# A language-model layer on one core: the score banks become a ring of three pairs, all other TensorE jobs share one PSUM bank, and the order of work is rewritten

## The chip, the core and the metric

The kernel runs on one core of a Trainium2 chip. Its engines work through queues of their own, each in order: TensorE (PE in the profile, its weight loads PEld), VectorE (DVE), ScalarE (ACT), GpSimd (POOL) and SyncE (SP, transfers only). They wait for one another through semaphores. The metric is the device time of one execution in microseconds, as the median of several runs.

## The reference

Inputs are token numbers (8, 1024), a segment label, tables, and the weights of one transformer layer of width 192, with 12 heads of 16 and a hidden width of 768.

```python
h = segment_row + position + token_row          # (8, 1024, 192)
x = layernorm(h)
q, k, v = split(x @ qkv_weight.T)               # 12 heads of 16
q, k = layernorm(q) * 16**-0.5, layernorm(k)    # over each head's 16
h = h + (softmax(q k^T) @ v) @ proj_weight.T    # 1024 x 1024 scores, 8 x 12 times
x = layernorm(h)
x = round(clip(x / mean(alpha_a1), -8, 7)) @ wq1.T   # quantised weights
x = clip(gelu(x * alpha_w1 * mean(alpha_a1) + b1), -10, 10)
x = round(clip(x / mean(alpha_a2), -8, 7)) @ wq2.T
h = h + x * alpha_w2 * mean(alpha_a2) + b2
```

## The kernel before

The 8 x 1024 positions are cut into 16 halves of 512 positions (`HALVES`), and each half into four tiles of 128 (`TH`). The kernel goes through a short start, 16 half-steps and a tail. Half-step s does the attention of the 512 queries of half s against all 1024 keys. It consists of 24 units: a unit (u) is one group of four heads with one tile of 128 keys. For each unit TensorE writes four score matrices (`scores`, L1212) in two pairs of PSUM banks (`ps_s`, four banks), ScalarE takes the Exp of each pair (`exps`, L679) into one of four buffers `probs`, and TensorE multiplies by v (`heads`, L1232) into the bank `ps_o`. That last step stands two units behind (`HEADS_BEHIND`). A pair of score banks is written again once its last Exp is done.

All other work is laid between the units by hand: the text `PLAN` (L77) has a line for each of the 24 units, and each engine reads from it, in order, the words that concern it. A word is a letter with the tile's number. Capital letters of `JOB_KINDS` are TensorE jobs that write a PSUM bank of their own, and VectorE copies or uses the result when its queue comes to the same word: A turns the normed input, B makes q and k, C makes v, D and E turn q and k, F turns the attention's output and divides it by the row sums, G turns it back, H projects it and adds it to h, I turns the quantised input, X is the first feed-forward product (then Gelu on ScalarE), Y the second, W turns weights (in half-step 1 alone). Further words are VectorE's own: P and l are row statistics, R the reciprocal roots of both of them in one chain of 11 small linked operations, N and m apply the norms, r sums squares, S takes the 96 roots for q and k, n splits q and k into high and low halves, x quantises a Gelu block, o copies `ps_o`. h stands for a unit of `heads` on TensorE, g marks the place of the six Gelus on ScalarE (`GELU_UNIT`), which loads the Gelu table before them and the Exp table after.

In half-step s these jobs work on different halves (`LAG`): P, N and A to E on half s+2, F to I and X on s-1, Y on s-2. So half-steps 1 to 13 have all of A to E, 14 and 15 have none.

The jobs go round three PSUM banks `ps_j` (`bank_of`, L208): X on two of them in turn, B on the third, the rest in the order of the plan. A job waits until the last result in its bank has been taken out (`job_before`, L220). PSUM has eight banks: 4 + 1 + 3.

GpSimd has its own fixed order in each half-step (`one`, L608):

```python
add_result(s0, s)            # waits for all four Y tiles, two additions
ahead = s0 + GATHER_AHEAD    # 3
if FIRST_GATHERED <= ahead < HALVES:     # half-steps 1 to 12
    add_segments(ahead)      # four gathers, then a wait for them to land
    add_tokens(ahead)        # four gathers
square(s0, s)                # for each tile: waits for B's copy; r waits for it
split_low(s0, s)             # low halves: waits for n; D and E wait for it
```

`link` makes VectorE wait until its own operation has finished, before the next that reads it.

## Time and profile before

| | |
|---|---|
| median of 3 runs | 1070.18 us (1068.22 to 1071.05) |
| span of the profiled execution | 1067.6 us, nothing beside it is listed |
| TensorE matmuls busy | 979.4 us (92%) |
| ScalarE busy | 872.6 us (82%) |
| VectorE busy | 813.9 us (76%) |
| GpSimd busy | 411.8 us (39%) |
| longest waits | TensorE's score weight loads for the Exp, 267.6 us in 420 waits; ScalarE's Exp for scores, 120.6 us in 183 |

Busy time of TensorE contains the overlap of matmuls in its pipeline, so 92% doesn't mean that it runs at its peak. The profile is of one execution, and the sums below are made against its span.

### The profile page before, as it was taken

The page shows a single profiled execution, that of the slowest core. Times are in us where ns is not written, and L with a number is a line of the kernel's source. Part 1 is how long each engine was busy: PE and PEld are TensorE (multiplying, and loading weights), DVE is VectorE, ACT ScalarE, POOL GpSimd, SP SyncE. Part 2 cuts the span into 40 slices and gives each one's busy share as a digit, 9 for nine tenths or more (in the row PEclk, how much of TensorE's full clock was granted, in tenths as well). Part 3 has the DMA queues.
Part 4 walks back from the last instruction along what each step waited for, and adds up shares of the span by engine and source line. Part 5 has one row for each costly group of instructions (what it writes and reads, how often), then busy time and mean ns, then how long its engine had stood idle before and what let it go on. Part 6 is the DMA issues. An engine that isn't in the chain of part 4 may idle for free.

```text
span 1067.6 us, 19577 instructions
## 1 busy us (share of the span) xinstructions
PE 979.4 (92%) x7571; PEld 389.1 (36%) x7571; DVE 813.9 (76%) x2325; ACT 872.6 (82%) x950; POOL 411.8 (39%) x345
## 2 busy tenths in 40 slices
PE   5589999999999999999999999999999999989885
PEld 4333433334342433434343343434334343413223
DVE  5878869788686969878696977869697886825347
ACT  1387788897979889797988979798888989798883
POOL 6555513635343353534435363443526412201000
PEclk9899999999999999999999999999999999999997
DMA  7511200303011040202102040110202000000000
GB/s 162 127 16 16 31 1 2 46 1 64 12 25 22 1 75 1 38 8 58 18 2 45 1 73 3 31 16 16 30 1 45 1 16 1 16 1 1 16 1 31
DMA packets 25762, 28.62 MB, mean 27 GB/s; under 512 B 5027, under 2 KB 22182, under 8 KB 25670
## 3 DMA queue, kind: packets, MB, share of 16 engines
q0 software_dynamic: 16896, 11.80, 9.4%
q1 hardware_dynamic: 8624, 15.55, 4.8%
q8 instruction: 61, 1.00, 0.4%
q14 instruction: 31, 0.25, 0.1%
q10 hardware_dynamic: 150, 0.01, 0.0%
HBM read 21.06 MB, written 6.29 MB: 26 GB/s over the span
## 4 chain that ended last, share of the span: by engine, by line
PE 40%; ACT 30%; DVE 24%; issue 3%; POOL 3%; DMA 0%
ACT probs L682 22%; PE ps_o L1247 12%; PE ps_s L1227 8%; PE ps_j L1271 4%; ACT gelu L676 4%; PE ps_j L1279 3%; PE ps_j L1325 3%; POOL stack L592 3%; PE ps_j L1286 2%; PE ps_j L1292 2%; ACT L676 2%; ACT L682 2%; DVE hn L797 2%; PE ps_j L1311 2%; PE ps_j L1296 2%
## 5 line engine op out<-in xcount | busy, mean ns | idle before, releaser
L682 ACT ACTIVATE probs<-ps_s 128x1024 f32<-128x1024 f32 x768 | 736.1, 1023 | 125.5 <-PE ps_s L1227 120.6
L1247 PE MATMUL ps_o<-probs,v_sb 128*32 128x512 f32 x3072 | 394.7, 605 | 0.2 <-DVE o_sb L859 0.2
L1227 PE MATMUL ps_s<-qT,kT 64*128 64x512 f16 x1536 | 264.3, 384 | 35.0 <-ACT probs L682 25.2
L592 POOL TENSOR_TENSOR stack<-sq,stack 128x384 f16<-128x384 f32 x124 | 120.5, 992 | 162.9 <-DVE stack L846 162.9
L1227 PEld LDWEIGHTS ps_s<-qT,kT 64*128 64x128 f16 x1536 | 61.5, 93 | 299.5 <-ACT probs L682 267.6
L525 POOL DMA_INDIRECT h_all<-in_L_tok_token_table,idx x60 | 96.7, 1611 | 59.5 <-DMA h_all<-in_L_tok_segm_table,idx 41.2
L1247 PEld LDWEIGHTS ps_o<-probs,v_sb 128*32 128x32 f32 x3072 | 69.1, 109 | 124.3 <-issue 116.1
L601 POOL TENSOR_TENSOR y_sb<-y_sb,b_row 128x768 f32<-128x768 f32 x14 | 25.4, 1814 | 198.8 <-DVE y_sb L931 198.8
L581 POOL TENSOR_TENSOR sq<-qk 128x384 f32<-128x384 f32 x56 | 46.2, 826 | 139.5 <-DVE qk L894 139.5
L525 POOL DMA_INDIRECT h_all<-in_L_tok_segm_table,idx x56 | 87.2, 1557 | 15.2 <-issue 13.1
L1279 PE MATMUL ps_j<-wh,partsT 128*128 128x384 f16 (+1 forms) x384 | 71.5, 296 | 1.0 <-ACT partsT L663 0.7
L1286 PE MATMUL ps_j<-ident_h,stack 128*128 128x128 f16 x768 | 61.2, 224 | 11.8 <-POOL stack L592 10.4
L676 ACT ACTIVATE gelu<-ps_j,b_sb,s_sb 128x512 f32<-128x512 f32 x90 | 65.3, 773 | 7.5 <-PE ps_j L1311 6.7
L894 DVE TENSOR_SCALAR qk<-ps_j,w_back 128x384 f32<-128x384 f32 x56 | 34.6, 618 | 48.1 <-PE ps_j L1279 48.0
L1286 PEld LDWEIGHTS ps_j<-ident_h,stack 128*128 128x128 f16 x768 | 45.6, 100 | 50.1 <-issue 39.3
L859 DVE COPY o_sb<-ps_o 128x512 f32<-128x512 f32 x47 | 32.0, 680 | 41.4 <-PE ps_o L1247 41.4
L846 DVE CAST stack<-sq 128x384 f16<-128x384 f32 x128 | 58.7, 500 | 2.2
L878 DVE TENSOR_SCALAR gelu<-gelu,ia,qlo 128x512 f32<-128x512 f32 x90 | 58.4, 648 | 0.0
L1311 PE MATMUL ps_j<-xqT,w1T 96*128 96x512 bf16 x180 | 52.9, 388 | 3.7 <-ACT gelu L676 2.7
L1279 PE MATMUL ps_j<-wl,partsT 128*128 128x192 f16 (+1 forms) x256 | 54.3, 295 | 0.0
L879 DVE TENSOR_SCALAR gelu<-gelu,qhi 128x512 f32<-128x512 f32 x90 | 50.8, 565 | 3.2
L1271 PE MATMUL ps_j<-wpT,oT 96*128 96x192 f32 x240 | 45.7, 333 | 0.0
(201 smaller groups left out, 1118.5 us busy)
## 6 DMA issues: line engine op xcount, KB each, us to landing
out<-h_all SPq DMA_DIRECT2D x15, 384.0 KB
h_all<-in_positions SPq DMA_DIRECT2D x7, 768.0 KB
gelu<-in_L_ffn_w SPq DMA_DIRECT2D x2, 576.0 KB
h_all<-in_L_tok_token_table,idx POOLq DMA_INDIRECT x60
h_all<-in_L_tok_segm_table,idx POOLq DMA_INDIRECT x56
probs<-in_L_attn_qkv_weight SPq DMA_DIRECT2D x2, 432.0 KB, 4.7
h_all<-in_positions SPq DMA_DIRECT2D x2, 384.0 KB, 8.0
o_nat<-in_L_ffn_alpha_a SPq DMA_DIRECT2D x1, 384.0 KB
```

What stands on the lines that cost most here:

```text
L525: nc.gpsimd.indirect_dma_start(out=h_tile(half, j), out_offset=None, in_=table, in_offset=bass.IndirectOffsetOnAxis(ap=idx[:, which, t:t + ...
L592: last = nc.gpsimd.tensor_tensor(low, src, high, ALU.subtract)
L676: nc.scalar.activation(gelu[:, j], bank(("X", j), s0), ACT.Gelu, bias=b1_sb[:, j:j + 1], scale=s1_sb[:, j:j + 1]).then_inc(job_out["X"], 1)
L682: nc.scalar.activation(probs[:, u % PROBS, 2 * pair:2 * pair + 2], ps_s[:, 2 * pair:2 * pair + 2], ACT.Exp, scale=SCORE_SCALE).then_inc(ex ...
L846: last = nc.vector.tensor_copy(high, src)
L878: link(ts(gelu[:, t], gelu[:, t], ia2[:], qlo[:], ALU.mult, ALU.max))
L1227: last = mm(ps_s[:, j], kT[rows, par, head // 2, m * P:(m + 1) * P], qT[rows, par, head // 2, nh * NQ:(nh + 1) * NQ], start=True, stop=True)
L1247: last = mm(ps_o[32 * j:32 * j + 2 * D, :], v_sb[:, par, m, (GH * group + j) * VE:(GH * group + j) * VE + 2 * D], probs[:, u % PROBS, j], ...
L1271: last = mm(ps[:, 0:C], oT[:, t, k], wpT[:, k], start=(k == 0), stop=(k == 1))
L1279: last = mm(ps[:, 0:hi - lo], partsT[:, t, m], w, start=(n == 0), stop=(n == len(passes) - 1))
L1286: last = nc.tensor.transpose(bank16((kind, t), s0, F16)[:, i * P:(i + 1) * P], src, ident_h[:])
L1311: last = mm(ps, w1T[:, k, t * P:(t + 1) * P], xqT[:, k], start=(k == 0), stop=(k == 1))
```

## The change

The eight PSUM banks are divided anew: 6 + 1 + 1. `ps_s` becomes a ring of three pairs. The pairs of scores and the three pairs of X (`hidden`) take its places in turn (`RING_ORDER`); `ring_free` makes an entry wait for the one three places before it. All other jobs share the single bank `ps_j` from half-step 1 on. Half-step 0 and the start keep three job banks (two of them lie in the ring's third pair) and their order.

Jobs are merged over tiles from half-step 1 on (`TILES`): A, C, G, H and Y do two tiles in one job with one copy, I all four; `count` converts the semaphore counts. The roots R are split into R for the first norm and Q for the second; the norms N and m are done in two halves each. The Gelus come one unit after the mark g. The plan is written anew.

```diff
 PLAN = """
-h h o
-Y0 Y1 Y2 F0 Y3 F1
-G0 F2 F3 H0 G1 P0
-h h
-G2 G3 W0 W1 W2 H1 H2 H3
-h l0 h R0
-W3 m0 h
-W4 h
-h N0 W5 I0
-I1 h o A0
-I2 h A1 A2
-h A3 I3
-C0 B0 X0
-X1 B1 r0 X2 X3 B2 X4 X5 r1 B3 h r2 h r3 g h
+h h o P0
+Y0 F0 R0
+h Y1 N0
+h F1 F2 N1
+h F3 A0
+h G0 A1
+h B0 r0 G1
+h B1 r1 W0
+H0 h W1
+h o B2 r2 W2
+h H1 W3
+h B3 r3 l0 W4
+h S0 W5
+h Q0 n0
+h m0 m1 C0
+h I0 n1 D0
+X0 h E0 n2 X1 D1 h X2 o g E1 n3 C1
+D2 x0 E2
+h D3 x1
+h E3 x2
+h x3
+h x4
+h x5
 h
-h S0 n0
-h n1 o
-D0 x0 E0 C1
-n2 h C2 D1
-E1 n3 h
-D2 h x1
-h D3 E2 x2
-E3 x3 x4 h
-x5 C3 h
 """
...
-JOBS = [w[:2] for unit in UNIT_WORK for w in unit if w[0] in JOB_KINDS]
-GELU_UNIT = next(u for u, unit in enumerate(UNIT_WORK) if ("g", 0, 0) in unit)
+JOBS = [w[:2] for unit in UNIT_WORK for w in unit if w[0] in JOB_KINDS and w[0] != "X"]
+GELU_UNIT = next(u for u, unit in enumerate(UNIT_WORK) if ("g", 0, 0) in unit) + 1
...
 BANKS = 3
-IN_TURN = [w for w in JOBS if w[0] not in "XB"]
+PAIRS = 3
+TILES = {"A": 2, "C": 2, "G": 2, "H": 2, "Y": 2, "I": 4}
+FIRST_MERGED = {"A": 3, "C": 3}
+LAST_MERGED = {"G": HALVES - 1, "H": HALVES - 1, "I": HALVES - 1, "Y": HALVES - 2}
+RING_ORDER = [entry for u in range(HG * TB)
+              for entry in ([("X", 0), ("X", 1), ("X", 2)] if u == GELU_UNIT else []) + [("S", 2 * u), ("S", 2 * u + 1)]]
...
 def bank_of(job, s0):
-    kind, t = job
-    if s0 <= 0:
-        return START_JOBS.index((job, s0)) % BANKS
-    return {"X": t % 2, "B": 2}[kind] if kind in "XB" else IN_TURN.index(job) % BANKS
+    return START_JOBS.index((job, s0)) % BANKS if s0 <= 0 else 0
...
+def tiles_of(kind, s0):
+    return TILES.get(kind, 1) if s0 >= 1 else 1
...
-        ps_s = ctx.enter_context(nc.psum_tensor("ps_s", [P, GH, NQ], F32))
+        ps_s = ctx.enter_context(nc.psum_tensor("ps_s", [P, 2 * PAIRS, NQ], F32))
         ps_o = ctx.enter_context(nc.psum_tensor("ps_o", [P, NQ], F32))
-        ps_j = ctx.enter_context(nc.psum_tensor("ps_j", [P, BANKS, 512], F32))
+        ps_j = ctx.enter_context(nc.psum_tensor("ps_j", [P, 512], F32))
+        def job_bank(n):
+            return (ps_j[:], ps_s[:, 4], ps_s[:, 5])[n]
...
+        def ring(s0, entry):
+            return entry[1] % 2 if s0 == 0 else RING_ORDER.index(entry) % PAIRS
...
-            def norm_roots(s0):
-                lo = 0 if job_runs("P", s0) else 1
-                hi = 2 if job_runs("H", s0) else 1
-                if lo < hi:
-                    rsqrt(rn[:, lo:hi], vn[:, lo:hi], wn[:, lo:hi])
-            def first_norm(s0, s):
+            def norm_roots(which):
+                rsqrt(rn[:, which], vn[:, which], wn[:, which])
+            def first_norm(s0, s, i):
                 half = job_half("N", s)
                 if s0 == -2:
@@ -793,12 +833,13 @@
                 if s0 <= 0:
                     dve.wait_ge(job_mm["A"], (s + 2) * TH)
-                for t in range(TH):
+                here = slice(0, TH) if s0 <= 0 else slice(2 * i, 2 * i + 2)
+                for t in range(TH)[here]:
                     last = ts(hn[:, t], h_tile(half, t), mv[:, 0, t, 0:1], rn[:, 0, t:t + 1],
                               ALU.subtract, ALU.mult)
                 link(last)
-                link(nc.vector.tensor_copy(parts[:, :, 0:C], hn[:]))
-                tt(parts[:, :, C:2 * C], hn[:], parts[:, :, 0:C], ALU.subtract).then_inc(hn_ready, 1)
+                link(nc.vector.tensor_copy(parts[:, here, 0:C], hn[:, here]))
+                tt(parts[:, here, C:2 * C], hn[:, here], parts[:, here, 0:C], ALU.subtract).then_inc(hn_ready, 1)
...
-            def second_norm(s0, s):
+            def second_norm(s0, s, i):
                 half = job_half("I", s)
-                link(ts(ra2[:], rn[:, 1], ia1[:], None, ALU.mult))
-                for t in range(TH):
+                if i == 0:
+                    link(ts(ra2[:], rn[:, 1], ia1[:], None, ALU.mult))
+                here = slice(2 * i, 2 * i + 2)
+                for t in range(TH)[here]:
                     last = ts(xf[:, t], h_tile(half, t), mv[:, 1, t, 0:1], ra2[:, t:t + 1],
                               ALU.subtract, ALU.mult)
                 link(last)
-                quantise(xq[:], xf[:], xf[:], QN, QP).then_inc(xq_ready, 1)
+                quantise(xq[:, here], xf[:, here], xf[:, here], QN, QP).then_inc(xq_ready, 1)
...
+                    two = h_all[:, at:at + 2 * C]
+                    tt(two, ps[:, 0:2 * C], two, ALU.add).then_inc(job_out["H"], 1)
...
+            def ring_free(s0, s, entry):
+                if s0 == 0:
+                    if entry[1] >= 2:
+                        pe.wait_ge(exp_done, entry[1] - 1)
+                    return
+                at = RING_ORDER.index(entry)
+                if at >= PAIRS:
+                    (kind, n), step = RING_ORDER[at - PAIRS], s
+                elif s0 >= 2:
+                    (kind, n), step = RING_ORDER[at - PAIRS], s - 1
+                elif at < 2:
+                    (kind, n), step = ("S", 2 * UNITS - 2 + at), s - 1
+                else:
+                    for bank_n in (1, 2):
+                        (pk, pt), step = [j for j in START_JOBS if bank_of(*j) == bank_n][-1]
+                        pe.wait_ge(job_out[pk], count(pk, job_half(pk, step), pt))
+                    return
+                if kind == "S":
+                    pe.wait_ge(exp_done, 2 * UNITS * step + n + 1)
+                else:
+                    pe.wait_ge(job_out["X"], count("X", job_half("X", step), 2 * n + 1))
...
+            def hidden(s0, s, i):
+                half = job_half("X", s)
+                if i == 0:
+                    pe.wait_ge(job_out["I"], count("I", half, TH - 1))
+                ring_free(s0, s, ("X", i))
+                for j in (2 * i, 2 * i + 1):
+                    for k in range(2):
+                        last = mm(ps_s[:, 2 * ring(s0, ("X", i)) + j % 2], w1T[:, k, j * P:(j + 1) * P], xqT[:, k],
+                                  start=(k == 0), stop=(k == 1))
+                    last.then_inc(job_mm["X"], 1)
```

The `nth(...)` counts in all waits on jobs become `count(...)`; the start's and the tail's uses of the banks go through `job_bank`. Start, tail and half-step 0 are otherwise as they were.

## Rows read from the trace of the kernel before

**Rows 1.** Timeline of ScalarE: start us, us, engine, operation
```profile
458.10 1.28 ACT L676 ACT_TABLE_LOAD   x1
...
464.25 1.28 ACT L682 ACT_TABLE_LOAD   x1
...
465.55 11.46 ACT L682 ACTIVATE probs<-ps_s 128x1024 f32<-128x1024 f32 x12
...
519.68 1.28 ACT L676 ACT_TABLE_LOAD   x1
```

**Rows 2.** Windows, one half-step: busy us of PE, PEld, DVE, ACT, POOL
```profile
458.10:519.68 61.58, 58.89 (x470) 22.86 (x468) 49.62 (x140) 52.92 (x56) 27.28 (x22) 1.00 0.18 33
```

**Rows 3.** Timeline of TensorE
```profile
463.03 0.66 PE L1279 MATMUL ps_j<-wh,partsT 128*128 128x384 f16 x3
...
463.95 2.78 PE L1247 MATMUL ps_o<-probs,v_sb 128*32 128x512 f32 x24
...
477.35 0.61 PE L1227 MATMUL ps_s<-qT,kT 64*128 64x512 f16 x4
...
477.88 0.51 PE L1286 MATMUL ps_j<-ident_h,stack 128*128 128x128 f16 x6
...
500.18 2.16 PE L1271 MATMUL ps_j<-wpT,oT 96*128 96x192 f32 x12
```

**Rows 4.** Groups of VectorE: count, busy us, mean ns, idle before
```profile
L894 DVE TENSOR_SCALAR qk<-ps_j,w_back 128x384 f32<-128x384 f32 x56 | 34.6, 618 | 48.1 <-PE ps_j L1279 48.0
...
L859 DVE COPY o_sb<-ps_o 128x512 f32<-128x512 f32 x47 | 32.0, 680 | 41.4 <-PE ps_o L1247 41.4
...
L918 DVE TENSOR_TENSOR o_nat<-ps_j,rsum 128x192 f32<-128x192 f32 x60 | 21.4, 357 | 2.1
```

**Rows 5.** Timeline of VectorE
```profile
466.20 0.21 DVE L831 TENSOR_SCALAR vq<-vq 128x96 f32<-128x96 f32 x1
...
469.57 0.56 DVE L841 TENSOR_TENSOR sq<-qk,rq 128x384 f32<-128x384 f32 x1
...
470.16 0.63 DVE L846 CAST stack<-sq 128x384 f16<-128x384 f32 x2
...
471.29 1.95 DVE L846 CAST stack<-sq 128x384 f16<-128x384 f32 x2
...
502.77 0.35 DVE L768 BATCH_NORM_STATS2 st<-h_all 128x6 f32<-128x192 f32 x1
...
504.86 0.17 DVE L745 TENSOR_SCALAR wn<-vn 128x8 int32<-128x8 int32 x1
...
507.43 1.25 DVE L870 TENSOR_SCALAR o_nat<-h_all,mv,ra 128x192 f32<-128x192 f32 x4
...
509.78 1.31 DVE L797 TENSOR_SCALAR hn<-h_all,mv,rn 128x192 f32<-128x192 f32 x4
```

**Rows 6.** Timeline of GpSimd
```profile
494.42 1.81 POOL L601 TENSOR_TENSOR y_sb<-y_sb,b_row 128x768 f32<-128x768 f32 x1 [11.10 <-DVE y_sb L931]
...
498.28 1.54 POOL L525 DMA_INDIRECT h_all<-in_L_tok_segm_table,idx  x1
...
508.83 1.84 POOL L525 DMA_INDIRECT h_all<-in_L_tok_token_table,idx  x1 [3.47 <-DMA h_all<-in_L_tok_segm_table,idx]
...
514.66 1.54 POOL L525 DMA_INDIRECT h_all<-in_L_tok_token_table,idx  x1 [0.30 <-issue]
...
520.35 0.82 POOL L581 TENSOR_TENSOR sq<-qk 128x384 f32<-128x384 f32 x1 [4.15 <-DVE qk L894]
```

**Rows 7.** Timeline and windows of TensorE, with the granted clock
```profile
28.11 0.48 PE L1299 MATMUL ps_j<-ident_h,parts 128*128 128x128 f16 x3 [9.59 <-DVE parts L791]
...
512.83 0.33 PE L1299 MATMUL ps_j<-ident_h,parts 128*128 128x128 f16 x3 [0.37 <-DVE parts L801]
...
30.00:35.00 5.00, 5.00 (x18) 2.54 (x19) 3.73 (x17) 2.62 (x6) 4.39 (x3) 1.00 1.10 246
...
45.00:50.00 5.00, 3.00 (x28) 2.52 (x26) 4.86 (x11) 1.93 (x3) 2.57 (x2) 0.50 0.04 15
```

More of the change, by code:

```diff
@@ L208, in bank_of, with count @@
 def bank_of(job, s0):
-    kind, t = job
-    if s0 <= 0:
-        return START_JOBS.index((job, s0)) % BANKS
-    return {"X": t % 2, "B": 2}[kind] if kind in "XB" else IN_TURN.index(job) % BANKS
+    return START_JOBS.index((job, s0)) % BANKS if s0 <= 0 else 0
+def count(kind, half, t):
+    per, tiles = PER_HALF[kind], TILES.get(kind, 1)
+    whole = min(half, FIRST_MERGED.get(kind, 0))
+    merged = max(min(half, LAST_MERGED.get(kind, HALVES)) - whole, 0)
+    rest = half - whole - merged
+    own = tiles if whole == FIRST_MERGED.get(kind, 0) and half < LAST_MERGED.get(kind, HALVES) else 1
+    return (whole + rest) * per + merged * (per // tiles) + t // own + 1
+def tiles_of(kind, s0):
+    return TILES.get(kind, 1) if s0 >= 1 else 1
 def jobs_of(s0):
@@ L576, in square @@
                 for t in range(TH):
-                    pool.wait_ge(job_out["B"], nth(half, t, TH))
+                    pool.wait_ge(job_out["B"], count("B", half, t))
                     if job_half("B", s0) > 2 or t >= 2:
@@ L656, in copy_out @@
                 half = job_half(kind, s)
-                act.wait_ge(job_mm[kind], nth(half, t, TH))
+                act.wait_ge(job_mm[kind], count(kind, half, t))
                 if kind == "B":
@@ L674, in gelu_out @@
                 half = job_half("X", s)
-                act.wait_ge(job_mm["X"], nth(half, j, HB))
-                nc.scalar.activation(gelu[:, j], bank(("X", j), s0), ACT.Gelu, bias=b1_sb[:, j:j + 1],
+                act.wait_ge(job_mm["X"], count("X", half, j))
+                nc.scalar.activation(gelu[:, j], ps_s[:, 2 * ring(s0, ("X", j // 2)) + j % 2], ACT.Gelu, bias=b1_sb[:, j:j + 1],
                                      scale=s1_sb[:, j:j + 1]).then_inc(job_out["X"], 1)
@@ L885, in job_result @@
                 half, h0 = job_half(kind, s), job_half(kind, s0)
-                job = (kind, t)
+                job, first = (kind, t), t * tiles_of(kind, s0)
                 ps = bank(job, s0)
@@ L890, in job_result @@
                         continue
-                    dve.wait_ge(job_mm[kind], nth(half, t, TH))
+                    dve.wait_ge(job_mm[kind], count(kind, half, first))
                     if kind in "BC":
@@ L1258, in job @@
                     (pk, pt), ps_step = prior
-                    pe.wait_ge(job_out[pk], nth(job_half(pk, ps_step), pt, PER_HALF[pk]))
+                    pe.wait_ge(job_out[pk], count(pk, job_half(pk, ps_step), pt * tiles_of(pk, ps_step)))
                 ps = bank((kind, t), s0)
+                tiles = range(t * tiles_of(kind, s0), (t + 1) * tiles_of(kind, s0))
                 if kind == "A":
@@ L1263, in job @@
                         pe.wait_ge(hn_first, t + 1)
-                    elif t == 0:
+                    elif s0 <= 0 and t == 0:
                         pe.wait_ge(hn_ready, half)
+                    elif s0 >= 1:
+                        pe.wait_ge(hn_ready, 2 + 2 * (half - 3) + t + 1)
                 if kind == "B":
-                    pe.wait_ge(job_out["A"], nth(half, t, TH))
+                    pe.wait_ge(job_out["A"], count("A", half, t))
                 if kind == "H":
-                    pe.wait_ge(job_out["G"], nth(half, t, TH))
-                    for k in range(2):
-                        last = mm(ps[:, 0:C], oT[:, t, k], wpT[:, k], start=(k == 0), stop=(k == 1))
+                    pe.wait_ge(job_out["G"], count("G", half, tiles[0]))
+                    for n, tile in enumerate(tiles):
+                        for k in range(2):
+                            last = mm(ps[:, n * C:(n + 1) * C], oT[:, tile, k], wpT[:, k], start=(k == 0), stop=(k == 1))
                 if kind in "BC":
@@ L1277, in job @@
                     passes = [(m, high[:, m]) for m in range(KP)] + [(m, low[:, m]) for m in range(KP - 1)]
-                    for n, (m, w) in enumerate(passes):
-                        last = mm(ps[:, 0:hi - lo], partsT[:, t, m], w, start=(n == 0), stop=(n == len(passes) - 1))
+                    for i, tile in enumerate(tiles):
+                        for n, (m, w) in enumerate(passes):
+                            last = mm(ps[:, i * C:i * C + hi - lo], partsT[:, tile, m], w,
+                                      start=(n == 0), stop=(n == len(passes) - 1))
                 if kind in "DE":
```

161 lines of the change are left out of this document (92 added, 69 removed).

## The prediction

> **What bounds the kernel now.** I read the windows first: one steady half-step. The two ScalarE table loads that open the Gelu blocks of two successive half-steps stand at 458.10 and 519.68 [rows 1], so a half-step takes 61.6 us. In it TensorE is busy 58.9, ScalarE 52.9, VectorE 49.6 and GpSimd 27.3 us [rows 2]. Then the timeline of ScalarE: a table load and six Gelus from 458.10 to 464.25, so the load 1.28 and the Gelus with their waits 4.9, table load 1.28, then Exps at 0.955 us each (twelve in 11.45) [rows 1]. 48 Exps and this block make 53, so ScalarE idles 8.6 us of 61.6. TensorE's rows carry the rest: four score matmuls 0.54 us (477.35 to the transposes at 477.88), the head matmuls of one unit (eight passes) 0.93 in a row (2.78 for three units), some 1.0 alone, a B job 0.9, three H tiles 2.1 [rows 3]. No one engine is full. The half-step is set by how four in-order queues interlock, so I ask of the new PLAN where each queue stands behind another one.
>
> **The change part by part.**
>
> *The ring of three score pairs.* PE may now write the scores of pair n once Exp n-3 is done, before n-2. That lets it run about one Exp (0.96 us) further ahead. It pays where PE jobs come in lumps: at most that 8.6 us of ScalarE idling, over 15 half-steps. It gives nothing where PE itself waits in its own queue, since the scores stand behind the waiting job.
>
> *One job bank.* Back-to-back jobs are serial: hand-over to VectorE 0.2, copy 0.6 (618 ns for 384 columns [rows 4]), hand-over back 0.15, so about 1 us of PE wait when nothing lies between. Twelve or so such neighbours stand in the new PLAN. Those after F1, F2, F3, G0 and B0 cost 4 to 5 us by this price, but two longer waits, below, take most of them in.
>
> *Merging.* Two tiles in one copy save 0.1 to 0.2 us on VectorE (2 x 357 ns for 192 columns against 618 for 384 [rows 4]), 1 to 2 us per half-step. A second root chain costs 2.3 us more (504.86 to 507.43, less 0.26 for the scaling at its end [rows 5]), halved norms 0.5. VectorE stays near 50 us: a draw. It matters only through the order.
>
> *The new order,* which carries the forecast. I walk one steady half-step as a closed path, time 0 being F0 on TensorE in unit 1.
>
> a) F0 0.33 and its VectorE part 0.6 (product 0.36 [rows 4], reciprocal and link 0.25) with hand-overs: 1.15. VectorE then does R0, 2.3, and only then copies Y1 (0.55): the last y is out at **4.0**.
>
> b) GpSimd works its queue in order: add_result, the eight gathers of a later half, and only then the squares. In the trace it starts adding at 494.42, when the last y is out; the segment gathers begin at 498.28, the token gathers at 508.83 after a wait for the former to land; the last begins at 514.66 and takes 1.54, so it is free at 516.2, 21.8 us after the last y [rows 6]. Before, the first square was wanted at 520.35, when GpSimd had already sat idle 4.15 us. In the new PLAN B0 and r0 stand in unit 6, four units after Y1. TensorE reaches the end of B0 at about 16 on my path (Y1 1.0, two F, A, G0 and five times scores and heads of 1.54, with the bank waits). The square can start only at 25.9. VectorE sits in r0, behind it the copy of G1, behind that, in the only job bank, B1. So r0 ends 21.8 + 0.8 square + 0.55 reduce + 0.2 = **23.35** later.
>
> c) Copy of G1 and hand-over: **0.8**.
>
> d) TensorE from B1 to the end of B3, units 7 to 11: three B 2.55, two merged H 2.8, four scores 2.2, four heads 4.0, bank wait between B1 and H0 0.35: **11.9**. ScalarE needs 7.7 for these four units, so PE leads.
>
> e) From B3's end to I0. VectorE's queue there is r3, l0, S0, Q0, n0, m0, m1, then the copy of C0, which frees the bank. Before, S0 started 2.25 us after B3's last matmul (463.95 to 466.20 [rows 5, 3]); l0 takes 2.1 (502.77 to 504.86), S0 3.4 (466.20 to 469.57), Q0 2.2, n0 1.15, m0 and m1 2.35 (507.43 to 509.78) plus 0.7 for the halving [rows 5], C0's copy and hand-over 0.75. Beside m0 GpSimd makes the low parts: such a pair of casts took 1.95 instead of 0.6 [rows 5], so 1.4 more. Sum **16.3**. Over it TensorE has four units of scores and heads and C0, 7.1 us, ScalarE 7.7: neither covers it. PE stands about 9 us at I0 and ScalarE runs dry, because the scores of unit 16 stand behind I0 and D0.
>
> f) I0 0.7, its copy and hand-overs 1.05, D0 0.45, scores to the first Exp 0.45, two Exps 1.95, table load, six Gelus, table load 7.0 (7.4 before, with 0.47 of waiting): **11.6**.
>
> g) Fourteen Exps, to the end of unit 23: **13.4**. PE has 1.5 to 1.9 us per unit against 1.92: ScalarE bounds, as in the long run after 465.55 [rows 1].
>
> h) Heads of unit 23 wait for the last Exp, 1.15; copy o 0.68 [rows 4], statistics P0 1.95, Y0's copy and hand-over 0.7: F0 may start after **4.5**. P0 before Y0's copy is new; it puts 2 us on the path.
>
> Sum: 4.0 + 23.35 + 0.8 + 11.9 + 16.3 + 11.6 + 13.4 + 4.5 = 85.9.
>
> *The clock.* In the steady half-step the granted clock is 1.00 [rows 2]. In the prologue PE stood 9.59 us before 28.11 and then needed 0.48 for three transposes that take 0.33 later; in 45 to 50 us, after the next gap, the clock is 0.50 [rows 7]. The path above has two gaps of some 9 us, in b and e. The rows show about 5 us of dense work at 1.2 GHz until it recovers. After b PE is on the path: +2.6. After e: I0, D0 and scores at half speed +1.7, and the last Gelu pair comes late by another 1.3: +3.0. Below, nothing (the clock may hold); above, double.
>
> So a half-step takes 91.5, 29.9 more than before. That holds for half-steps 2 to 12, eleven of them: +329. Half-step 13 gathers nothing: r0 follows B0 at once, 9.0 less in b and no clock loss of 2.6: +18. Half-step 1 adds no result, and its gathers are early enough: +18 too, and the six W jobs, each in the one bank with a 0.68 copy, +5. Half-steps 14 and 15 have no A to E and none of b's or e's queue: the ring gains some 2 us each, -4. Half-step 0 and the tail keep their order: 0. 1067.6 + 329 + 18 + 23 - 4 = 1433.6, and 2.6 for the median of the runs over this span: **1436**.
>
> The Trainium skill, in "SBUF — State Buffer", section "Who interferes with whom", says that VectorE's two-port operations and GpSimd exclude each other for a whole instruction, whoever comes first. By that rule m0's first operations would wait one or two GpSimd subtractions, 0.9 to 1.8 us in place of my 1.4. The trace agrees in size: +1.35 for the pair of casts [rows 5].
>
> The same skill, in "PSUM — Partial Sum Buffer", section "Summary: rules for kernel authors", advises to write a different bank while one is read. It speaks against the single job bank. By the row's turnaround of 1 us, twelve neighbours would cost up to 12 us per half-step and the time would be at most 1250 if that were all; the two queues in b and e are dearer and cover most of it.
>
> **Rivals.** *The clock holds* over the two gaps: 11 x 5.6 + 2 x 3 = 68 less, 1368. For it: the windows of 25 to 35 us, whose matmuls were slow, are listed at full clock [rows 7], so the link between gap and speed is loose. *GpSimd's queue is no wait*: TensorE comes to B0 so late, or the gathers start so early, that the squares are ready. Then b shrinks to 14.35 and 11 x (9.0 + 2.6) = 128 fall away: 1308. Against: add_result waits for Y1 itself, so only a stretch Y1 to B0 of 22 us would do it. *Both queues are longer*: VectorE's operations beside the gathers, or half speed for 10 us: up to 11 x 5.6 more, 1500. *Faster*: the waits of b and e are covered, the third pair evens the lumps out and only TensorE's 58.9 us [rows 2] count: 2.7 x 14 = 38 less, 1032. It decides if Y1 to B0 plus the VectorE queue of e shrink by over 24 us; ScalarE's idle 8.6 us speak for a gain, the two queues against it. *The change does nothing to the pace*: excluded but for chance, since the order itself changes.
>
> **Numbers.** Forecast 0.58; clock holds 0.17; GpSimd hidden 0.08; longer 0.08; somewhere between 1080 and 1290 by overlaps I missed 0.03; faster 0.05; same 0.01. The range 1290 to 1490 takes in the first three and part of the fourth, 0.85. The measurement tells about 0.3%, 3 us, from no change. Slower 0.94, same 0.01, faster 0.05.
>
> **What would show it.** Right: Gelu loads about 91 us apart in the middle, near 80 for half-steps 1 and 13, 60 or less in the last two; VectorE waiting 8 to 9 us in the reduce of r0 for the square, once per half-step; GpSimd with no idle time between its last gather and its first square; ScalarE idle over 8 us twice per half-step; clock at 0.5 in windows after the gaps. Wrong: a GpSimd square that waits for qk as before, an I0 that starts within 10 us of B3, or a steady clock.

## The result and the profile after

| | before | after |
|---|---|---|
| median of the runs | 1069.3 us (1068.2 to 1071.1) | 1418.3 us (1412.2 to 1421.2, 4 runs) |
| profiled execution, span | 1067.6 us | 1419.5 us |
| granted clock of TensorE, mean | 0.983 | 0.88 |

The ratio is 1.325, 95% interval 1.321 to 1.329: 349 us slower. The window of one half-step of the changed kernel, between two Gelu table loads (busy us of PE, PEld, DVE, ACT and POOL, then the granted clock), answers to [rows 2]:

```profile
540.10:629.75 89.65, 67.16 (x469) 23.95 (x468) 52.10 (x141) 52.58 (x57) 26.49 (x22) 0.86 0.10 14
```

The half-step is 28.1 us longer. ScalarE and GpSimd are busy about as long as before (52.6 and 26.5 us) and VectorE 2.5 us longer. TensorE is busy 8.3 us longer over practically the same matmuls (469 and 470); its granted clock is 0.86 where it was 1.00. The other 20 us are waits. ScalarE's timeline shows where (the idle time before a row in brackets; compare [rows 1]):

```profile
566.57 1.94 ACT L725 ACTIVATE probs<-ps_s 128x1024 f32<-128x1024 f32 x2 [1.70 <-PE ps_s L1299]
...
576.23 1.94 ACT L725 ACTIVATE probs<-ps_s 128x1024 f32<-128x1024 f32 x2 [5.09 <-PE ps_s L1299]
...
595.27 1.94 ACT L725 ACTIVATE probs<-ps_s 128x1024 f32<-128x1024 f32 x2 [5.69 <-PE ps_s L1299]
...
627.79 1.94 ACT L725 ACTIVATE probs<-ps_s 128x1024 f32<-128x1024 f32 x2 [10.82 <-PE ps_s L1299]
629.75 1.28 ACT L718 ACT_TABLE_LOAD   x1
...
636.98 1.28 ACT L725 ACT_TABLE_LOAD   x1
```

In its three longest waits for scores (5.09, 5.69 and 10.82 us) TensorE itself stands still, each time for VectorE. TensorE's timeline (compare [rows 3] for B, H and the scores at full speed):

```profile
565.66 0.55 PE L1370 MATMUL ps_j<-ident,o_sb 128*128 128x128 f32 x3 [1.45 <-DVE y_sb L976]
...
574.75 0.90 PE L1370 MATMUL ps_j<-ident,o_sb 128*128 128x128 f32 x3 [3.90 <-DVE o_nat L961]
...
592.90 1.14 PE L1356 MATMUL ps_j<-wh,partsT 128*128 128x384 f16 x3 [4.09 <-DVE oT L939]
...
595.58 2.93 PE L1347 MATMUL ps_j<-wpT,oT 96*128 96x192 f32 x8
...
605.06 1.57 PE L1347 MATMUL ps_j<-wpT,oT 96*128 96x192 f32 x8
...
609.01 0.60 PE L1299 MATMUL ps_s<-qT,kT 64*128 64x512 f16 x4
...
624.52 1.09 PE L1386 MATMUL ps_j<-ident_b,xq 128*96 128x128 bf16 x8 [8.32 <-DVE v_sb L937]
```

These are F0, F2, B1, H0, H1, the scores behind B3, and I0. The reason for the gap at B1 is read from GpSimd's timeline (compare [rows 6]) and then VectorE's:

```profile
569.59 1.88 POOL L643 TENSOR_TENSOR y_sb<-y_sb,b_row 128x768 f32<-128x768 f32 x1 [20.60 <-DVE y_sb L976]
...
573.50 1.54 POOL L567 DMA_INDIRECT h_all<-in_L_tok_segm_table,idx  x1
...
583.75 1.53 POOL L567 DMA_INDIRECT h_all<-in_L_tok_token_table,idx  x1 [3.16 <-DMA h_all<-in_L_tok_segm_table,idx]
...
589.27 1.54 POOL L567 DMA_INDIRECT h_all<-in_L_tok_token_table,idx  x1 [0.30 <-issue]
590.25 1.42 POOL L623 TENSOR_TENSOR sq<-qk 128x384 f32<-128x384 f32 x1
```

```profile
569.43 2.16 DVE L838 TENSOR_SCALAR hn<-h_all,mv,rn 128x192 f32<-128x192 f32 x2
571.63 1.94 DVE L841 CAST parts<-hn 128x384 f16<-128x384 f32 x1
...
576.23 0.73 DVE L838 TENSOR_SCALAR hn<-h_all,mv,rn 128x192 f32<-128x192 f32 x2
576.99 0.36 DVE L841 CAST parts<-hn 128x384 f16<-128x384 f32 x1
...
591.70 0.55 DVE L865 TENSOR_REDUCE vq<-sq 128x24 f32<-128x384 f32 x1 [5.12 <-POOL sq L623]
592.17 0.68 DVE L939 COPY oT<-ps_j 96x512 f32<-96x512 f32 x1
```

GpSimd squares only when its eight gathers are through; VectorE waits 5.12 us in r0 with the copy of G1 behind it, and B1 waits for that copy. The first two rows (N0) against the next two (N1) also show a wait that the prediction did not have: beside GpSimd's two additions, N0 took 4.1 us for what N1 does in 1.1. F1's copy stands behind N0 in VectorE's queue, and F2 needs the one bank that this copy frees, hence F2's 3.90 us.

Over the whole program: the Gelu loads of half-steps 2 and 12 stand at 274.66 and 1168.38, 89.4 us per half-step against 61.6. The Gelus stand five units later in the new order, so for single half-steps I count from the first Exp of one to the first Exp of the next. By that measure the 352 us between the two spans are 24 in half-step 1 (87.4 against 63.4), 307 in half-steps 2 to 12 (984.2 against 677.6 together), 20.5 in half-step 13 (81.6 against 61.1) and less than 1 in half-steps 14 and 15 together. Half-step 0 and the tail take as long as before.

### The profile page after: what moved, and what is told of

It is laid out like the page before. It is cut to its first block, busy times and chain, and to the rows that moved or that the text cites. A ratio compares the mean times of both kernels' runs of the same rounds, so it can differ in the third digit from the quotient of the medians.

```text
span 1419.5 us, 19572 instructions
## 1 busy us (share of the span) xinstructions
PE 1079.6 (76%) x7571; PEld 399.3 (28%) x7571; DVE 843.1 (59%) x2339; ACT 866.9 (61%) x950; POOL 402.9 (28%) x345
## 4 chain that ended last, share of the span: by engine, by line
PE 39%; DVE 27%; POOL 15%; ACT 9%; issue 9%; DMA 1%; POOLq 0%; DVEq 0%
PE ps_o L1319 13%; POOL h_all L567 10%; ACT probs L725 8%; PE ps_s L1299 6%; PE ps_j L1347 4%; PE ps_j L1364 4%; PE ps_s L1414 4%; PE ps_j L1356 4%; DVE o_nat L913 2%; DVE st L811 2%; POOL sq L623 2%; DVE stack L887 2%; DVE sq L882 2%; POOL y_sb L643 1%; POOL h_all L647 1%
## 5 line engine op out<-in xcount | busy, mean ns | idle before, releaser
L1319 PE MATMUL ps_o<-probs,v_sb 128*32 128x512 f32 x3072 | 434.8, 645 | 1.3 <-DVE o_sb L900 0.8
L634 POOL TENSOR_TENSOR stack<-sq,stack 128x384 f16<-128x384 f32 x124 | 113.1, 933 | 312.3 <-DVE stack L887 312.3
L1299 PEld LDWEIGHTS ps_s<-qT,kT 64*128 64x128 f16 x1536 | 51.1, 95 | 210.9 <-ACT probs L725 144.3
L1386 PE MATMUL ps_j<-ident_b,xq 128*96 128x128 bf16 x120 | 15.4, 305 | 105.2 <-DVE v_sb L937 105.2
L1370 PE MATMUL ps_j<-ident,o_sb 128*128 128x128 f32 x180 | 38.2, 329 | 69.0 <-DVE o_nat L961 50.3
L865 DVE TENSOR_REDUCE vq<-sq 128x24 f32<-128x384 f32 x56 | 31.0, 553 | 95.4 <-POOL sq L623 95.4
L937 DVE TENSOR_SCALAR qk<-ps_j,w_back 128x384 f32<-128x384 f32 x54 | 33.4, 618 | 75.3 <-PE ps_j L1356 75.3
L718 ACT ACTIVATE gelu<-ps_s,b_sb,s_sb 128x512 f32<-128x512 f32 x90 | 64.2, 774 | 14.3 <-PE ps_s L1414 14.0
L939 DVE COPY kT<-ps_j 128x768 f16<-128x768 f16 x54 | 30.0, 556 | 63.0 <-PE ps_j L1364 63.0
L1347 PE MATMUL ps_j<-wpT,oT 96*128 96x192 f32 x240 | 60.2, 406 | 1.1 <-DVE w1T L946 0.9
L1356 PEld LDWEIGHTS ps_j<-wh,partsT 128*128 128x128 f16 x342 | 26.4, 101 | 118.3 <-DVE oT L939 56.8
```

The source lines that it names most:

```text
L634: last = nc.gpsimd.tensor_tensor(low, src, high, ALU.subtract)
L718: nc.scalar.activation(gelu[:, j], ps_s[:, 2 * ring(s0, ("X", j // 2)) + j % 2], ACT.Gelu, bias=b1_sb[:, j:j + 1], scale=s1_sb[:, j:j + 1] ...
L1299: last = mm(ps_s[:, at], kT[rows, par, head // 2, m * P:(m + 1) * P], qT[rows, par, head // 2, nh * NQ:(nh + 1) * NQ], start=True, stop=True)
L1319: last = mm(ps_o[32 * j:32 * j + 2 * D, :], v_sb[:, par, m, (GH * group + j) * VE:(GH * group + j) * VE + 2 * D], probs[:, u % PROBS, j], ...
L1347: last = mm(ps[:, n * C:(n + 1) * C], oT[:, tile, k], wpT[:, k], start=(k == 0), stop=(k == 1))
L1356: last = mm(ps[:, i * C:i * C + hi - lo], partsT[:, tile, m], w, start=(n == 0), stop=(n == len(passes) - 1))
```

## The experiments

Every run is compared with the kernel before on the same chip. All keep the whole computation.

**1. The gathers last in GpSimd's queue**, to take the squares out from behind them.

```diff
                 add_result(s0, s)
                 ahead = s0 + GATHER_AHEAD
+                square(s0, s)
+                split_low(s0, s)
                 if FIRST_GATHERED <= ahead < HALVES:
                     add_segments(ahead)
                     add_tokens(ahead)
-                square(s0, s)
-                split_low(s0, s)
```

> The changed kernel with one edit: GpSimd does its squares and low halves ahead of the gathers of a later half. The order theory says that VectorE's reduce r0 in unit 6 stands behind the gathers in half-steps 2 to 12. Without that wait B1 starts some 8 us earlier, and what TensorE does at half speed behind that gap is gained too, about 4 us: 11 x 12 = 130 us less, near 1285. The rival that the single job bank sets the pace says that r0 only fills time in which jobs would wait anyway: under 2% less, above 1390. If the gathers at the end hold up the next add_result or P0, some 3 us per half-step come back, near 1320.

Measured: 1435.6 us, ratio 1.343 (1.338 to 1.347): slower than the change itself. The squares come at once (first row), but the wait did not go, it moved. VectorE's, GpSimd's and TensorE's timelines:

```profile
595.86 0.55 DVE L865 TENSOR_REDUCE vq<-sq 128x24 f32<-128x384 f32 x1 [0.94 <-POOL sq L623]
...
659.29 0.35 DVE L811 BATCH_NORM_STATS2 st<-h_all 128x6 f32<-128x192 f32 x1 [5.94 <-issue]
```

```profile
654.90 1.54 POOL L567 DMA_INDIRECT h_all<-in_L_tok_token_table,idx  x1 [0.30 <-issue]
```

```profile
661.69 0.90 PE L1370 MATMUL ps_j<-ident,o_sb 128*128 128x128 f32 x3 [7.46 <-DVE y_sb L976]
```

GpSimd is through with the last token gather at 656.4, and P0's first row starts at 659.29. The profile names no releaser for that wait; I read it as the landing of the tokens, some 3 us later. P0 of the next half-step needs them and, new in this order, stands ahead of Y0's copy. So GpSimd's queue has two deadlines: squares by unit 6 and tokens by P0. The expectation had named the second one, but at some 3 us; the wait is 5.94 us. The time also lies above the rival's 1390, but not for its reason, as run 5 shows.

**2. TensorE kept at work in the gaps** of half-steps 1 to 13 by extra score matmuls (20 before F2, 24 before B1, 48 before I0), overwritten by the real scores.

```diff
+            WARM = {("F", 2): (4, 20), ("B", 1): (8, 24), ("I", 0): (16, 48)}
...
                         elif kind in job_mm:
+                            if at is None and 1 <= s0 <= 13 and (kind, t) in WARM:
+                                warm(s0, s, *WARM[kind, t])
```

> The changed kernel with score matmuls done ahead of time, and again at their place, while TensorE would stand idle: 20 ahead of F2, 24 ahead of B1, 48 ahead of I0, in half-steps 1 to 13. They fill most of the gaps and fit in them. If the half speed behind the gaps is a cost of its own, the matmuls from B1 to B3 take 12 instead of 16 us and those from I0 on 2 us less: 60 to 80 us less in all, 1340 to 1360, with a granted clock near 1. If the clock is only a sign and VectorE and GpSimd set the pace, the time stays within 1% of 1418. If the added matmuls delay the jobs behind them, it rises by up to 30.

Measured: 1392.8 us, ratio 1.307 (1.298 to 1.316), clock 0.955 in the profiled execution: 25 us faster than the change, less than expected. The four times spread more than in other runs, from 1388.5 to 1407.4. From B1 to the scores behind B3 it took 13.8 us (581.21 to 594.97) against 16.1. TensorE's timeline shows why not more:

```profile
575.73 2.76 PE L1415 MATMUL ps_s<-qT,kT 64*128 64x512 f16 x24
581.21 0.66 PE L1356 MATMUL ps_j<-wh,partsT 128*128 128x384 f16 x3 [2.71 <-DVE oT L939]
...
582.90 2.81 PE L1347 MATMUL ps_j<-wpT,oT 96*128 96x192 f32 x8 [0.17 <-DVE qk L937]
...
594.97 0.61 PE L1299 MATMUL ps_s<-qT,kT 64*128 64x512 f16 x4
...
610.47 1.09 PE L1386 MATMUL ps_j<-ident_b,xq 128*96 128x128 bf16 x8 [3.02 <-DVE v_sb L937]
```

The fillers left 2.71 and 3.02 us of gap, and H0 and I0 behind them still ran at half speed. So the clock has at least these 25 of the 349 us. It can't be the main cause: with a clock of 0.955, 323 us were left.

**3. The order of the change on nearly the old division of PSUM**: two score pairs and three job banks.

```diff
-PAIRS = 3
+PAIRS = 2
...
-    return START_JOBS.index((job, s0)) % BANKS if s0 <= 0 else 0
+    return START_JOBS.index((job, s0)) % BANKS if s0 <= 0 else JOBS.index(job) % BANKS if job in JOBS else 0
...
-        ps_j = ctx.enter_context(nc.psum_tensor("ps_j", [P, 512], F32))
+        ps_j = ctx.enter_context(nc.psum_tensor("ps_j", [P, BANKS, 512], F32))
```

One thing differs from the kernel before: X stays in the ring, beside the scores, while before it had job banks of its own.

> The changed kernel's order, merging and roots, with PSUM divided as before: two pairs in the ring (scores and X share it) and three job banks in turn. The order theory says that the division of PSUM is a minor part: B1 may pass the blocked copy of G1, I0 the copy of C0, some 5 us per half-step, against a little less lead of the scores: 1340 to 1400. If the single bank were the cause, most of the 350 us would go: under 1200.

Measured: 1395.2 us, ratio 1.304 (1.302 to 1.307). With the third pair given up for two more job banks, the kernel is 23 us faster; no run separates what the banks gain from what the pair loses. The ring is not what made the kernel slow. The Trainium skill advises to write another bank while one is read ("PSUM — Partial Sum Buffer", section "Summary: rules for kernel authors"): the runs agree in this order, by these 23 us net; run 8 shows the opposite sign in another.

**4. VectorE's queue ahead of I0 shortened**: l0, r3, Q0, C0, m0, m1, I0 ahead of S0 and n0 (units 11 to 15, each line of the plan put between bars), and the D and E jobs about one place later.

```diff
-h B3 r3 l0 W4 | h S0 W5 | h Q0 n0 | h m0 m1 C0 | h I0 n1 D0
+h B3 l0 r3 W4 | h Q0 C0 W5 | h m0 m1 I0 | h S0 | h n0 n1
...
```

> The changed kernel with VectorE's queue behind B3 in another order: l0 ahead of r3, Q0, C0's copy, m0, m1 and I0 ahead of S0 and n0, and the D and E jobs one place later. The order theory: from B3 to I0 9 to 10 us in place of 15.5, and S0 and n0 lie beside I0 and three units, so 5 to 6 us less in each of 13 half-steps: 1340 to 1350. The rival that VectorE is simply full over the half-step, so that moving its work about gives nothing: within 1% of 1418.

Measured: 1404.8 us, ratio 1.313 (1.307 to 1.318): 13.5 us faster, a fifth of the expected. From B3's end to I0 it is now 8.9 us (686.2 to 695.14) instead of 15.5, as meant. But the Exps of units 14 and 15 now come behind I0 and not ahead of it, and D0 to E1, pushed behind the Gelus, make ScalarE wait 2.22 and 1.43 us there. ScalarE still idles 5.7 us at I0, and half-steps 14 and 15, which have no A to E, got 7 us longer together (from first Exp to first Exp, 123.2 against 116.0):

```profile
628.03 1.94 ACT L725 ACTIVATE probs<-ps_s 128x1024 f32<-128x1024 f32 x2 [2.22 <-PE ps_s L1299]
631.40 1.94 ACT L725 ACTIVATE probs<-ps_s 128x1024 f32<-128x1024 f32 x2 [1.43 <-PE ps_s L1299]
...
696.78 1.94 ACT L725 ACTIVATE probs<-ps_s 128x1024 f32<-128x1024 f32 x2 [5.72 <-PE ps_s L1299]
```

**5. GpSimd's queue as add, segments, squares, tokens, low halves**: both deadlines of run 1 are met. The wait for the segments to land stands at the head of `add_tokens` in the code (and not at the end of `add_segments`, as the listing of GpSimd's order above has it), so the squares don't stand behind it.

```diff
                     add_segments(ahead)
+                square(s0, s)
+                if FIRST_GATHERED <= ahead < HALVES:
                     add_tokens(ahead)
-                square(s0, s)
                 split_low(s0, s)
```

> The changed kernel with GpSimd's queue cut otherwise: the addition, the segment gathers, the squares, then the token gathers, then the low halves. The segment gathers fit ahead of B0, the tokens between r3 and n0, so neither r0 nor the P0 of the next half-step should find GpSimd busy. The order theory: what putting all gathers last took from r0 and gave back at P0 is now kept, 8 us and some of the half-speed work per half-step, eleven times: 1290 to 1320. The rival, that r0's wait only covers other waits (the single bank, VectorE's queue): above 1390.

Measured: 1336.3 us, ratio 1.249 (1.246 to 1.252): 82 us faster than the change, though 16 us above the expected range, and 82.0 us per half-step. GpSimd's, VectorE's and TensorE's timelines (the last two rows are B1 and the scores behind B3):

```profile
629.24 1.54 POOL L567 DMA_INDIRECT h_all<-in_L_tok_segm_table,idx  x1 [0.30 <-issue]
636.80 0.83 POOL L623 TENSOR_TENSOR sq<-qk 128x384 f32<-128x384 f32 x1 [6.03 <-DVE qk L938]
```

```profile
637.67 0.55 DVE L866 TENSOR_REDUCE vq<-sq 128x24 f32<-128x384 f32 x1 [0.94 <-POOL sq L623]
```

```profile
638.89 0.66 PE L1357 MATMUL ps_j<-wh,partsT 128*128 128x384 f16 x3
...
651.02 0.60 PE L1300 MATMUL ps_s<-qT,kT 64*128 64x512 f16 x4
```

GpSimd now waits for the qk and not the other way round, and B1 to B3 take 12.1 us at full speed. This one place in the queue costs 82 us, and a time over 1390 us, which the rival gave, is refuted.

**6. Run 5 with P0 behind Y0's copy.**

```diff
-h h o P0
-Y0 F0 R0
+h h o
+Y0 P0 F0 R0
```

> As the run with the tokens behind the squares, and P0 one word later, behind Y0's copy. The statistics of 1.95 us then run beside scores and F0's wait and not ahead of Y0's copy: 1 to 2 us less in each of 13 half-steps, 13 to 26 us under that run. If VectorE's whole queue up to Y1 is what counts, P0 costs the same in either place: no difference.

Measured: 1351.4 us, ratio 1.263 (1.260 to 1.266), 15 us slower than run 5, which neither expectation had. In run 5, P0 lay beside Y0's matmuls, so it did not hold Y0's copy by its full length; behind it, it holds F0's. From the copy o to the copy of Y1 it took 6.3 us there (612.84 to 619.16) and 6.6 here (616.39 to 622.97), and F2 waits 4.62 instead of 3.90 us. So the prediction's term h (P0 ahead of Y0's copy puts 2 us on the path) named the right row but not a saving: GpSimd's addition hangs on Y1, and P0 is ahead of Y1's copy either way. Every second or third half-step is some 2.5 us longer than the others; why is not shown.

**7. Another spread order on the ring of three pairs and the one bank**, with GpSimd's queue of run 5, as in all runs that follow. The units 0 to 23, eight to a line:

```
h Y0 P0 | h | o Y1 | F0 h F1 h F2 | h R0 F3 | h | G0 h G1 N0 h H0 W0 | N1 H1 W1
A0 l0 | h B0 h W2 | o A1 Q0 h | B1 m0 r0 W3 | h B2 m1 W4 | r1 h W5 | B3 h r2 r3 | I0 S0 h
X0 h C0 n0 X1 C1 n1 X2 g h h x0 D0 | o E0 n2 | D1 h x1 | E1 n3 h | D2 h x2 E2 x3 | h D3 | h | x4 E3 x5 h
```

> The changed kernel's ring, single job bank, merging and split roots, with the tokens behind the squares and a new PLAN that spreads the jobs over the units, so that no queue stands behind a long chain of another: l0 in unit 8, Q0 in 10, m0 and m1 in 11 and 12, I0 in 14, S0 behind it, P0 and R0 in units 0 and 4. If the order is the cause and the division of PSUM and the merging cost nothing by themselves, a half-step takes 59 to 62 us and the time lies between 1030 and 1080, beside 1069. If one job bank, however well spaced, holds the jobs up, or VectorE is too full with two root chains, it stays above 1120.

Measured: 1114.6 us, ratio 1.042 (1.040 to 1.043), between the two expectations. It is 35 us above the first, but 304 of the 349 us are gone with the ring, the one bank, the merged jobs and the roots per norm all in place. What is left shows in TensorE's and VectorE's timelines:

```profile
501.70 0.82 PE L1365 MATMUL ps_j<-ident_h,stack 128*128 128x128 f16 x6 [2.99 <-DVE qT L940]
...
504.17 1.94 PE L1320 MATMUL ps_o<-probs,v_sb 128*32 128x512 f32 x8
```

```profile
493.36 0.55 DVE L883 TENSOR_TENSOR sq<-qk,rq 128x384 f32<-128x384 f32 x1
...
495.07 2.88 DVE L883 TENSOR_TENSOR sq<-qk,rq 128x384 f32<-128x384 f32 x1
...
498.53 0.54 DVE L922 TENSOR_SCALAR gelu<-gelu,ia,qlo 128x512 f32<-128x512 f32 x1
499.10 1.02 DVE L923 TENSOR_SCALAR gelu<-gelu,qhi 128x512 f32<-128x512 f32 x1
500.15 1.02 DVE L924 TENSOR_SCALAR hq<-gelu 128x512 bf16<-128x512 f32 x1
501.10 0.54 DVE L940 COPY qT<-ps_j 128x768 f16<-128x768 f16 x1
```

The copy of D0 stands behind n1, whose multiply takes 2.88 us instead of 0.55 beside two subtractions of GpSimd, and behind x0, slowed too. Then TensorE runs at half speed (0.82 us for six transposes that take 0.51 at 507.00, 1.94 for heads that take 1.07 at 507.44).

**8. Run 7 with two pairs and three job banks** (edit of run 3, order of run 7).

> The same new PLAN with PSUM divided as before: a ring of two pairs with X in it, and three job banks. It tells what the third pair is worth when no long wait stands in the way. If the ring evens out lumps of TensorE work, this is slower than the run with three pairs by 1 to 3 us per half-step, 15 to 45 us. If job banks matter more, it is faster.

Measured: 1148.1 us, ratio 1.073 (1.070 to 1.075): with X in the ring, three pairs with one bank are 33.5 us faster than two pairs with three banks in this order. It is not the division of the kernel before, whose X had job banks; no run tests that one in this order.

Counted from first Exp to first Exp, two parts of runs 3 and 8 have the same sign in both orders. In half-steps 14 and 15, without A to E, the third pair wins: 120.5 us with two pairs against 116.0 in the order of the change, and 121.6 against 113.3 in this one. In half-step 1, which has the W jobs besides, three job banks win: 76.3 against 87.4 us, and 68.7 against 75.3. Only in between does the sign hang on the order.

**9. Run 7 with D0's copy ahead of x0**, and **10. a third order**:

```diff
-X0 h C0 n0 X1 C1 n1 X2 g h h x0 D0
+X0 h C0 n0 X1 C1 n1 X2 g h h D0 x0
```

```
h | h o Y0 | F0 h F1 | F2 P0 h | G0 h | R0 Y1 h | F3 h G1 W0 | N0 H0 N1 h H1 W1
A0 h l0 | A1 h W2 | o B0 | h Q0 B1 m0 W3 | h B2 h W4 | r0 m1 B3 W5 | r1 r2 h I0 | r3 S0 h
X0 C0 X1 n0 C1 h X2 g | n1 D0 h x0 h E0 | o D1 | n2 E1 h | h x1 D2 h n3 | E2 h x2 | D3 h | x3 E3 x4 h x5
```

> The new order (1114.6 us) with two words exchanged: the copy of the first transposed Q (job D0) stands ahead of the first block of the Gelu's scaling (x0) in VectorE's queue. Theory: in each of the 13 middle half-steps TensorE waits 2.99 us for that copy, which is ready some 2.3 us earlier than VectorE comes to it, and then works at half speed for the next ~5 us (transposes of 0.82 instead of 0.51 us, heads of 1.94 instead of 1.06). With the copy ahead the gap falls under 1.5 us, the half speed goes, and a half-step is 2 to 3 us shorter: 1074 to 1092 us. Rival: the gap moves to the next wait of the same chain (the second multiply of the scaling, which takes 2.9 us beside GpSimd's low halves), or the order is close to its floor elsewhere: 1105 to 1115 us.

> The same kernel with another spread order of the same jobs (the transposes of the attention output one unit earlier, the first B job three units later, D0 ahead of x0, the words at most four in a unit but for one). It asks how much hangs on a particular order once the chain is spread. If what costs the 45 us over the kernel before is crowding at a few units, this order, whose units are more even, gives 1085 to 1110 us; if any spread order loses the same to GpSimd's and VectorE's shared reads, it gives 1110 to 1130 us.

Measured: run 9 1107.5 us, ratio 1.036 (1.034 to 1.038); run 10 1102.5 us, 1.031 (1.029 to 1.032). Run 9 lies in its rival's range: the gap before the second transposes shrank to 0.43 us, but the next link of the chain, x0 ahead of E0's copy, holds D1 by 2.35 us. Run 10 lies in its range of "crowding". TensorE's longest gap in the half-step from 423.72 is 1.02 us and the clock is 1.00 (half-steps 2 to 12 take 63.7 us each); the largest idle time of ScalarE, 2.90 us, lies where unit 7 holds H0, H1 and a head.

**11. A fourth order**, evened out by those two profiles:

```
h P0 Y0 h o Y1 | F0 h F1 | G0 | h R0 H0 | F2 h F3 | N0 G1 N1 h | H1 h A0 W0 | h l0 B0 h Q0 W1
B1 r0 | h A1 r1 W2 | o B2 m0 r2 | h B3 m1 W3 | r3 S0 h W4 | C0 h W5 | h n0 | h I0
h X0 n1 C1 g X1 X2 x0 h D0 h o E0 | n2 D1 h | x1 E1 | n3 h D2 x2 | h E2 | x3 h D3 | x4 h E3 | x5 h
```

> One more spread order of the same jobs on the ring of three pairs and the one bank: F and G drawn over six units, the H jobs in units 3 and 6, the square roots of the norm between other work, the Gelus one unit later, and D0 to E3 over the eight last units. Queues worked through from the durations of the last two runs (transposes 0.50 us, B 0.92, H 1.50, Gelu's inputs 1.00, heads 1.00, Exp 0.955; the second multiply of the scaling 3.2) give a half-step of 61.8 us where the last run had 63.7 and the kernel before has 61.6. Theory (the ring and the merged jobs cost nothing by themselves, only their order does): 1068 to 1085 us. Rival (the ring itself, which ties the Gelu's inputs to the Exps' pace, and the one bank leave a loss that no order removes): 1095 to 1115 us.

Measured: 1088.3 us, ratio 1.017 (1.016 to 1.019), between the two expectations. One half-step's window, against [rows 2]:

```profile
424.32:486.25 61.93, 58.94 (x469) 21.39 (x468) 53.01 (x142) 52.06 (x57) 27.27 (x23) 1.00 0.12 20
```

61.93 us, TensorE busy 58.94, clock 1.00: before it was 61.58 and 58.89. The steady loss is gone but for 0.35 us. From the first Gelu load to the last it takes 859.9 us (176.63 to 1036.56), before 857.7. Of the other 18 us, 15 lie in half-step 1 (78.5 us from first Exp to first Exp, before 63.4). There TensorE waits twice for the copy of a W job, and once a W job waits for the copy of B0 in the same bank:

```profile
148.47 0.72 PE L1357 MATMUL ps_j<-wh,partsT 128*128 128x384 f16 x3 [2.10 <-DVE w1T L947]
...
159.88 0.79 PE L1397 MATMUL ps_j<-ident,gelu 96*128 96x96 f32 x4 [1.35 <-DVE qk L938]
...
166.67 0.66 PE L1357 MATMUL ps_j<-wh,partsT 128*128 128x192 f16 x3 [3.10 <-DVE w2T L952]
```

**12. Run 11 with the W jobs in units 0 to 4** (W0 and W1 in unit 0, then one each).

> The tuned order (1088.3 us) with the six jobs that turn the feed-forward weights, which run in half-step 1 alone, moved from units 6 to 13 to units 0 to 4, where half-step 1 has no result (Y) to make. The last run's middle half-steps take 61.9 us, as good as the 61.6 of the kernel before, and from the first Gelu's table load to the last both take 858 to 860 us; its 18 us over the kernel before must lie in half-step 1, where TensorE waits 2.1, 1.35 and 3.1 us for those jobs' copies and VectorE's queue holds the B jobs up behind them. Theory: the jobs in one bank compete with the six extra ones there; ahead of them they cost little: 1076 to 1084 us. Rival: half-step 1 is long for another reason (the start's heads and the scaled weights arrive late, so the whole spread order waits at its first link): 1086 to 1092 us.

Measured: 1083.5 us, ratio 1.013 (1.012 to 1.015), at the end of the expected range. The theory holds in part: the three waits above are gone and half-step 1 takes 74.1 instead of 78.5 us, but that is still 10.7 us more than before. W1 now waits 3.90 us for W0's copy, which stands behind P0 and o in VectorE's queue, and runs at half speed (1.09 us for four transposes that take 0.64 ahead of the gap):

```profile
125.63 1.09 PE L1394 MATMUL ps_j<-ident,gelu 128*96 128x128 f32 x4 [3.90 <-DVE w1T L947]
```

What the rest of half-step 1 hangs on is not shown; run 8 against run 7 speaks for the one bank. Run 12 is the best version with all parts of the change, and still 1.3% behind the kernel before. No run beat that.

## Why the prediction was right

The forecast, 1436, is 1.2% over the measured 1418.3, inside the range, and on the right side. By its own steps, for the half-step with F0 at 565.66 (one of the longer ones: half-steps 2 to 12 take 86.9 to 91.9 us, 89.5 in the mean):

| step | forecast | measured |
|---|---|---|
| a, F0 to the last y | 4.0 | 3.9 (to 569.52) |
| b, GpSimd's queue to the end of r0 | 23.35 | 22.7 (to 592.25) |
| c, G1's copy | 0.8 | 0.65 (to 592.90) |
| d, B1 to B3, with the clock | 14.5 | 16.1 (to 609.01) |
| e, VectorE's queue to I0 | 16.3 | 15.5 (to 624.52) |
| f, I0 to the first Exp, with the clock | 14.6 | 13.75 (to 638.27) |
| g and h, Exps, heads, o, P0, Y0's copy | 17.9 | 18.2 (to 656.50) |
| sum | 91.5 | 90.8 |

- **b** was right in place and size, and run 5 proves it causal: freeing the squares alone gives 82 us. Before, GpSimd had sat idle 4.15 us ahead of the square; now the square starts as the last gather ends, as the sign of being right had it. But the VectorE wait was forecast as 8 to 9 us and was 5.12: B0 ended 20.3 us behind F0 and not 16, because N0 beside GpSimd's additions had already held F2 3.9 us. The path does not see it, since GpSimd's queue runs meanwhile. So the gathers were overpriced: without them the forecast had 79.9 us per half-step (11.6 less) and a time of 1308; run 5 has 82.0 and 1336, 7.5 less per half-step. In the sum the second error makes up for half of the first, which is luck.
- **e** was right in length and in the 8.3 us wait at I0; run 4 shows that shortening it alone saves 1 us per half-step, not the expected 6, because the same work comes back behind the Gelus.
- **The clock** was a mis-sized term. The forecast had some 5 us of half speed after each gap; [rows 7] show a window at 0.50, but not how long it takes to recover. Windows of the changed kernel, granted clock third from the right:

```profile
592.00:602.00 10.00, 9.10 (x33) 3.68 (x37) 2.58 (x5) 2.98 (x4) 0.82 (x1) 0.50 0.04 6
602.00:607.00 5.00, 5.00 (x37) 2.06 (x29) 2.20 (x4) 2.84 (x4) 0.83 (x1) 1.00 0.02 3
```

  After B1's gap half speed (1.2 GHz) lasts 10 us, and d takes 16.1 us (H0 takes 2.93 where H1 takes 1.57). Run 5, where B1 follows no long gap, takes 12.1 for the same stretch, so the bare 11.9 was right and the clock costs 4.0 there, not 2.6. f is 2.15 over its bare 11.6, not 3.0, but no run shows that 11.6 by itself. The sum, some 6.2 against 5.6, is nearly the same.
- **One job bank** was priced at 1 us for each pair of neighbours (0.2 and 0.15 for the two hand-overs, which no row gave); A0 behind F3 and G1 behind B0 waited 0.72 and 0.71 us in all (at 579.57 and 586.64), and run 3 puts the whole of it, net of the third pair, at 23 us.
- **The ring and the merged jobs as a gain** (the forecast's 8.6 us of ScalarE idle, and 2 us in each of half-steps 14 and 15): half-steps 14 and 15 were not shorter than before in the changed kernel (116.0 against 115.3 us), and 2.0 us shorter in run 7 (113.3). Run 8 against run 7 gives 33.5 us for three pairs and one bank against two pairs and three banks, but no run gained against the kernel before. The steady half-step of run 11, the best of four spread orders, is 61.93 against 61.58 us, with TensorE busy 58.9 us in both. That another order would gain is not excluded.
- **The totals**, from first Exp to first Exp: half-steps 2 to 12 took 27.9 us more each, where 29.9 was forecast, so 307 for eleven instead of 329; half-step 1 took 24 more where 23 was forecast, half-step 13 20.5 where 18 was, and the last two 0.7 where -4 was.
- **The signs**: the Gelu loads were 88 to 91 us apart in the middle, 81.3 into half-step 13 ("near 80") and 58.6 and 58.4 at the end ("60 or less"). Three signs failed: VectorE's wait in r0 was 5.12 us and not 8 to 9, the distance behind half-step 1's load was 91.6 and not near 80, and ScalarE idled over 8 us only once per half-step (10.82, at I0; at B1 it was 5.69, and 5.09 at F2).
- **The rivals.** "The clock holds" is refuted (0.88 in the mean). "GpSimd hidden" is refuted for this order; run 5 makes its condition true by other means, and lands at 1336 where the rival had 1308. "Both queues are longer" had one of its two conditions met, half speed for 10 us, behind the first gap; behind the second it was some 8 (from I0 at 624.52 to transposes at 631.80, 0.82 us for six), and step f came out below its forecast even so. "Faster" needed an order in which b and e shrink by 24 us; runs 7 to 12 are such orders (run 8 on the other division), and even they stop at 1.013. The gain it counted on, TensorE busy all the time, is not there: about 3 us per half-step stay idle in run 11.
